# A QKV block on one core: where an image is split, where raw heads lie, and who writes the constants

## The reference, cut to what matters

```python
x = x + _L0_conv_ref(_ln_c(x), w_qkv, w_proj, temperature)
# in it, for each head:
qkv = einsum('oc,bcs->bos', w_qkv, xf)      # q, k, v of 32 channels for each of 8 heads
q, k = _l2norm(q), _l2norm(k)
attn = softmax(einsum('bhsd,bhtd->bhst', q, k) * temperature)
out = einsum('bhst,bhtd->bhsd', attn, v)
```

## Time and profile before

| | |
|---|---|
| median of 3 runs | 2443.84 us |
| the profiled execution: its own time | 2460.1 us |
| its span | 2458.3 us |
| busy share of the span | PE 82%, DVE 84%, ACT 71%, POOL 26% |
| granted TensorE clock, mean over the span | 0.904 of full |
| TensorE's first projection to its last, about | 24 to 134 us |
| first scores of the attention | 167.58 us |

### The profile page before, as it was taken

How to read it: one execution, slowest core, us unless ns; L and a number is a source line. 1 busy time by engine, 2 the same in 40 slices (tenths; PEclk the granted TensorE clock), 3 DMA queues, 4 the chain that set the end, 5 groups by cost and what they waited for, 6 DMA issues and landing times. The chain is left out here.

```text
span 2458.3 us, 84235 instructions
## 1 busy us (share of the span) xinstructions
PE 2004.6 (82%) x28694; PEld 1522.9 (62%) x28695; DVE 2066.0 (84%) x3804; ACT 1751.1 (71%) x2771; POOL 635.1 (26%) x604
## 2 busy tenths in 40 slices
PE   6649999999999999999996307865897209999995
PEld 3327666666666666666665205652586209999995
DVE  5879999999999999999997746768798547888883
ACT  5669999999999999999994524546687426666662
POOL 3431111111111111111110463440164642333331
PEclk9869999999999999999998558995898559999997
DMA  2013232323232323232332233434022452223235
GB/s 82 1 34 91 74 89 73 90 73 90 72 91 72 91 71 91 71 92 71 92 89 73 83 126 116 116 93 146 30 69 76 160 177 46 49 47 49 50 49 152
DMA packets 296697, 203.12 MB, mean 83 GB/s; under 512 B 153587, under 2 KB 277958, under 8 KB 296358
## 3 DMA queue, kind: packets, MB, share of 16 engines
q1 hardware_dynamic: 275840, 163.70, 24.5%
q0 software_dynamic: 19776, 35.73, 5.6%
q10 hardware_dynamic: 998, 2.62, 0.3%
HBM read 64.79 MB, written 112.92 MB: 72 GB/s over the span
## 5 line engine op out<-in xcount | busy, mean ns | idle before, releaser
L595 DVE TENSOR_TENSOR plow<-prob 128x1024 f16<-128x1024 f32 (+1 forms) x1024 | 1128.1, 1173 | 4.7 <-ACT prob L506 4.7
L506 ACT ACTIVATE prob<-scores 128x1024 f32<-128x1024 f32 x1024 | 998.9, 1026 | 91.3 <-PE scores L638 63.6
L658 PEld LDWEIGHTS outp<-vs,prob 128*128 128x128 bf16 x7680 | 516.1, 98 | 277.9 <-issue 215.8
L658 PE MATMUL outp<-vs,prob 128*128 (+1 forms) x7680 | 604.2, 193 | 27.2 <-DVE plow L595 16.5
L638 PE MATMUL scores<-qT,kT 128*128 (+1 forms) x2048 | 611.6, 380 | 7.6 <-DMA kT<-shift_rows 2.7
L660 PE MATMUL outp<-vs,plow 128*128 (+1 forms) x7680 | 601.6, 193 | 0.0
L660 PEld LDWEIGHTS outp<-vs,plow 128*128 128x128 f16 x7680 | 503.3, 97 | 59.8 <-issue 0.6
L448 POOL TENSOR_TENSOR osum<-osb 128x128 f32<-128x128 f32 x64 | 85.8, 1341 | 968.3 <-DVE rec L600 968.3
L1527 POOL DMA_INDIRECT token_sums<-m1eyo,m1edest x71 | 132.4, 1864 | 292.9 <-DMA token_sums<-m1eyo,m1edest 183.6
L1370 PE MATMUL m1eph<-m1exT,m1ew1c 128*128 128x128 f16 x3408 | 204.3, 220 | 1.7 <-issue 1.7
L1370 PEld LDWEIGHTS m1eph<-m1exT,m1ew1c 128*128 128x128 f16 x3408 | 195.4, 99 | 2.4 <-ACT m1exT L1407 1.9
(11 more groups left out here) (398 smaller groups left out, 3375.2 us busy)
## 6 DMA issues: line engine op xcount, KB each, us to landing
sorted_rows<-zero SPq DMA_DIRECT2D x128, 522.0 KB, 5.0
staged<-qk SPq DMA_DIRECT2D x73, 128.0 KB, 2.3
m0exr<-sorted_rows SPq DMA_DIRECT2D x71, 130.5 KB
m1exr<-sorted_rows SPq DMA_DIRECT2D x71, 130.5 KB, 2.5
ls_got<-expert_rows SPq DMA_DIRECT2D x8, 1024.0 KB, 5.7
na_staged<-in_L_ffn_W_dram SPq DMA_DIRECT2D x16, 512.0 KB, 3.7
m1dstg<-in_L_ffn_W_dram SPq DMA_DIRECT2D x16, 512.0 KB
tok<-in_x_dram SPq DMA_DIRECT2D x8, 512.0 KB, 8.2
```

What stands on the lines that cost most here:

```text
L506: act.activation(prob[g % PBUF][:, :], scores[g % 2][:, :], ACT.Exp, scale=1.0 / (QK_SCALE * QK_SCALE)).then_inc(prob_ready, 1)
L595: dve.tensor_tensor(l[:, 0:n], p[:, 0:n], high(p)[:, 0:n], ALU.subtract).then_inc(low_ready, 1)
L658: pe.matmul(to, high(prob[g % PBUF])[:, cols], v, start=(g == 0 and i == 0 and j == 0), stop=False, skip_group_check=True)
```

## The change

1. The two blocks of constants are gone. Their GpSimd work is done at the start of `make_qkv`'s block, together with `zero` and the quarter of `qT`, now filled by one memset of 8192 elements a row. `qT`, `shift_rows` and `zero` are allocated outside the attention. VectorE makes `shift_rows` between the weights' centring and their split, and `tau` is loaded ahead of the image.
2. `raw` and `sq` no longer have memory of their own: they lie in the image's place. So all eight chunks must be split before the first `take`. ScalarE waits for `xl_ready` to reach `NG`.
3. `x_high` and `x_low` have left the loop. `heads_high(g - 1)` stands between tile 1 and tile 2 of group g.
4. The exponential's table is loaded by an instruction at the end of the block and no longer at the start of the attention.
5. In `layer1_start` the seven DMAs go from ScalarE's queue to the front of SyncE's.

```diff
-        raw = [sb(f"raw{u}", [P, GT, QK]) for u in range(2)]
-        sq = [sb(f"sq{u}", [P, GT, QK]) for u in range(2)]
+        image = xc[:, :, :].rearrange("p k s -> p (k s)").rearrange("p (n t c) -> p n t c", n=4, t=GT)
+        raw = [image[:, u] for u in range(2)]
+        sq = [image[:, 2 + u] for u in range(2)]
...
             sp.dma_start(wn[:, :, :], w_dram.rearrange("(m p) c -> p m c", p=P)).then_inc(w_in, 16)
+            sp.dma_start(tau[:, :], temp_dram.rearrange("h a b -> (h a b)").partition_broadcast(P)).then_inc(t_in, 16)
             for g in range(NG):
                 sp.dma_start(xc[:, :, chunk(g)], src[:, :, chunk(g)]).then_inc(x_in[g], 16)
-            sp.dma_start(tau[:, :], temp_dram.rearrange("h a b -> (h a b)").partition_broadcast(P)).then_inc(t_in, 16)
...
-            for g in range(EARLY):
-                x_high(g)
+            x_high(0)
             for n, (k, m0, m1) in enumerate(W_PARTS):
                 act.wait_ge(w_turned, n + 1)
                 act.activation(wh[:, k, m0 * P:m1 * P], pt[n % 2][:, 0:(m1 - m0) * P], ACT.Copy, scale=W_SCALE
                                ).then_inc(w_high, 1)
+                if n % 2:
+                    x_high(n // 2 + 1)
+            for g in range(3, NG):
+                x_high(g)
             act.wait_ge(made, 1)
             root(0)
+            act.wait_ge(xl_ready, NG)
             for g in range(NG):
                 if g >= 2:
                     act.wait_ge(q_low, (g - 1) * GT)
                     act.wait_ge(ss_ready, g - 1)
                 for i in range(GT):
+                    if g and i == GT // 2:
+                        heads_high(g - 1)
                     take(g, i)
                 if g + 1 < NG:
                     root(g + 1)
-                if EARLY <= g + 3 < NG:
-                    x_high(g + 3)
-                if g:
-                    heads_high(g - 1)
                 norms(g)
             heads_high(NG - 1)
+            act.activation(warm[:, :], tau[:, 0:1], ACT.Exp)
...
+            dve.wait_ge(t_in, 16)
+            dve.tensor_scalar(shift[:, :], tau[:, :], -1.0, None, ALU.mult).then_inc(shifted, 1)
...
+                pool.wait_ge(set_up, 10)
+                pool.memset(qT[3 * DH:4 * DH, :], QK_SCALE / DH).then_inc(set_up, 1)
+                pool.wait_ge(set_up, 11)
...
             pool.memset(vs[:, :, :, 2 * DH:VW], 1.0).then_inc(made, 1)
-            for g in range(EARLY):
+            constants()
+            for g in range(NG):
                 x_low(g)
             for g in range(NG):
-                if EARLY <= g + 3 < NG:
-                    x_low(g + 3)
                 heads_low(g)
```

More of the change, by code:

```diff
@@ L61, in clear_semaphores, with make_qkv @@
     nc.all_engine_barrier()
[L64 to L80, removed]
+def make_qkv(nc, x_dram, w_dram, temp_dram, ident32, ident16, consts, xc, wn, tau, qk, vs, qT, shift_rows, zero):
     assert QK_SCALE == W_SCALE
@@ L88, in make_qkv @@
     NV = 4
-    EARLY = 3
+    below, ones, steps, first, tile_no, tok2, base = consts
     ctx = ExitStack()
@@ L120, in make_qkv @@
         made = sem("made")
+        ident_zero = sem("ident_zero")
+        ident_done = sem("ident_done")
+        set_up = sem("set_up")
+        shifted = sem("shifted")
         xh_ready = sem("xh_ready")
@@ L276, in _ @@
                 dve.tensor_scalar(wn[:, m, :], wn[:, m, :], wmean[:, m:m + 1], None, ALU.add).then_inc(w_cent, 1)
+            dve.wait_ge(t_in, 16)
+            dve.tensor_scalar(shift[:, :], tau[:, :], -1.0, None, ALU.mult).then_inc(shifted, 1)
+            dve.wait_ge(shifted, 1)
+            dve.tensor_tensor(shift[:, :], shift[:, :], tau[:, :], ALU.max).then_inc(shifted, 1)
+            dve.wait_ge(shifted, 2)
+            dve.tensor_scalar(shift[:, :], shift[:, :], -1.0, P_SHIFT * LN2, ALU.mult, ALU.add).then_inc(shifted, 1)
+            dve.wait_ge(shifted, 3)
+            dve.tensor_scalar(shift_rows[3 * DH:4 * DH, :, :], shift[3 * DH:4 * DH, :].unsqueeze(2)
+                              .broadcast_to([DH, HEADS, CHUNK]), QK_SCALE, None, ALU.mult).then_inc(shifted, 1)
             for n, (k, m0, m1) in enumerate(W_PARTS):
@@ L310, in _ @@
+            pool.memset(ident32[:, :], 0.0).then_inc(ident_zero, 1)
+            pool.memset(ident16[:, :], 0.0).then_inc(ident_zero, 1)
+            pool.wait_ge(ident_zero, 2)
+            for m in (ident32, ident16):
+                pool.affine_select(out=m[:, :], in_=m[:, :], compare_op=ALU.not_equal, fill=1.0,
+                                   base=0, pattern=[[-1, P]], channel_multiplier=1).then_inc(ident_done, 1)
             pool.memset(vs[:, :, :, 2 * DH:VW], 1.0).then_inc(made, 1)
-            for g in range(EARLY):
+            constants()
@@ L364, in _, with attention @@
                     turn(g + 2)
-def attention(nc, qk, vs, tau, ident16, aout, sorted_rows):
+def attention(nc, qk, vs, ident16, aout, sorted_rows, qT, shift_rows, zero):
     ctx = ExitStack()
@@ L457, in _ @@
             pool.sem_inc(osb_used, 1)
-            pool.wait_ge(shift_set, 1)
-            for n in range(QCONST):
-                c = slice(n * 2 * S // QCONST, (n + 1) * 2 * S // QCONST)
-                pool.memset(qT[3 * DH:4 * DH, c], QK_SCALE / DH).then_inc(q_const, 1)
-            pool.wait_ge(q_const, QCONST)
             pool.memset(vfull[:, :, :, DH:DH + 1], 1.0).then_inc(vfull_set, 1)
@@ L480, in _ @@
         def _(act):
-            act.activation(warm[:, :], tau[:, 0:1], ACT.Exp)
             for j in range(NCH):
@@ L574, in _ @@
                 dve.sem_inc(placed[u], 16)
-            dve.tensor_scalar(shift[:, :], tau[:, :], -1.0, None, ALU.mult).then_inc(shift_ready, 1)
-            dve.wait_ge(shift_ready, 1)
-            dve.tensor_tensor(shift[:, :], shift[:, :], tau[:, :], ALU.max).then_inc(shift_ready, 1)
-            dve.wait_ge(shift_ready, 2)
-            dve.tensor_scalar(shift[:, :], shift[:, :], -1.0, P_SHIFT * LN2, ALU.mult, ALU.add).then_inc(shift_ready, 1)
-            dve.wait_ge(shift_ready, 3)
-            dve.tensor_scalar(shift_rows[3 * DH:4 * DH, :, :], shift[3 * DH:4 * DH, :].unsqueeze(2)
-                              .broadcast_to([DH, HEADS, CHUNK]), QK_SCALE, None, ALU.mult).then_inc(shift_set, 1)
             def take_turned(turn, u):
@@ L2215, in build @@
             wn = flat[:, NT * HEADS * 2 * DH - WN:NT * HEADS * 2 * DH].rearrange("p (m c) -> p m c", c=D)
-            make_qkv(nc, x, w_qkv, temperature, ident32, ident16, image, wn, tau, qk, vs)
-            attention(nc, qk, vs, tau, ident16, image, sorted_rows)
+            make_qkv(nc, x, w_qkv, temperature, ident32, ident16, consts, image, wn, tau, qk, vs, qT, shift_rows, zero)
+            attention(nc, qk, vs, ident16, image, sorted_rows, qT, shift_rows, zero)
         project_attention(nc, x, w_proj, image, ident32, tok, stats)
```

83 lines of the change are left out of this document (34 added, 49 removed).

## The result

The changed kernel took 2436.39 us (median of 18 runs, 2433.09 to 2443.88) against 2442.66 (18 runs, 2436.66 to 2450.08) of the kernel before on the same chip: a ratio of 0.9974, 95% interval 0.9964 to 0.9983. So it is 6 us faster, half of what I called the bound for telling a change, but measured twice. My sum said +1.7 us. The traced execution of the kernel before (2460.1 us) lies above all 18 of its runs here and among those on the other chips (2453.78 to 2472.84), while that of the changed kernel (2435.69) lies among its 18.

The account below looks back on a forecast made before the run. No engine was full in the loop; ScalarE's takes waited for GpSimd and TensorE. QKV block +3.3, attention's start -2.0 and layer 1 +0.4 gave +1.7 us: 2445.5 on the runs' median, range 2433.5 to 2452.5, with scatter 2455.

Parts of the forecast that it names:

- the bound for telling a change: Whole kernel: 0.5% (12.2 us), about what a measurement can tell from no change.
- The start: QKV block up to the first `take`: it comes at 41.0, 15.0 us later than before.
- The first four takes: QKV block, group 0: given 8.10 us, not the 5.9 that group 0 took at full clock.
- A round: QKV loop, norms to norms: 3.45 + 4.12 + 1.33 + 4.19 = 13.1 us; the seventh 11.5.
- The attention's start: Eight turns ahead of the attention: 10.3 us in place of 12.32, without memsets holding VectorE's copies; -2.0 us.
- Layer 1: Layer 1's start: SyncE's rows up to 3.8 us later, weights sooner; bounds 0 and +2, taken as +0.4 us.
- the sum of the QKV block: QKV block: last group's line 266 at 145.25 against 141.92, nothing changed from there to the block's end; +3.3 us.
- both rivals together: No lock at the start and no held units in the loop: 2432.6 us; chance 0.10.
- The rival that the lock does not bite at the start: Start: weights centred before the memset ends, low halves done at 35.1, 5.9 us less: 2439.6; chance 0.20.
- the one on the units: Loop: scalings not held by GpSimd, four take 2.50 us, round 12.1, 7 us less: 2438.5; chance 0.14.
- the rival of still later weights: Start: `tau` delays the image or centring is held six times; up to 4 us more, 2449.5; chance 0.06.
- the clock rival: Loop: TensorE stays at 1.2 GHz after pauses, 17.3 us a round, 2475 us, slower; chance 0.08.

Follow-up runs that it names:

- the run with the memset late: Changed kernel with the long memset of `qT` moved behind the image's last low half; ratio 0.9967 to the kernel before.
- the order alone: Kernel before with only the rounding of the heads moved between the second and third tile of the next group; ratio 0.9952 to the kernel before.

## Why the prediction was wrong

The sum said +1.7; the traces say -4.1 against the mean of the kernel before (3.8 at the first scores, 0.3 in layer 1), the time -6.3. By its own steps:

- **The start.** "+15.0 us" was 13.2. The mechanism is as written: the hold of the means' scaling to the memset's end, the held centring, then GpSimd's pace. Two sizes were off: the memset (8.2 for 6.92) and with it all that follows, and GpSimd's last low half at 39.1 for 41.0.
- **The first four takes.** I gave 8.10 because TensorE had stood idle; they took 6.96 (39.16 to 46.12), 1.1 us less. Two tiles were ready both times; the difference is the clock behind the third. In the earlier trace rows the fourth take came 2.90 us after the third, here 1.95, as in the second trace of the kernel before (56.40 to 58.35), where the clock was 1.00 from 56 us. Windows of the kernel before, then of the changed one (granted clock third from the right):

```profile
56.00:58.00 2.00, 2.00 (x9) 1.04 (x8) 1.03 (x3) 1.36 (x3) 0.00 (x0) 0.58 0.00 0
```

```profile
44.00:46.00 2.00, 2.00 (x16) 1.23 (x14) 0.35 (x1) 1.45 (x3) 0.00 (x0) 1.00 0.00 0
```

- **A round.** 13.1 was 12.85. Each part is where I put it: 3.30 us from norms to line 260 (76.00 to 79.30, forecast 3.45), four scalings in 3.46 held once, 4.1 from the first scaling to the last rounding's end (79.30 to 83.43). Over six rounds the quarter microsecond makes 1.5 us. These three make the 4.6 us by which line 260 came before my 145.25.
- **The reference.** I compared with line 266 at 141.92 in one trace. In the three others it starts at 143.16, 143.26 and 144.37. Another 1.3 us against the mean. My sum took one execution's QKV block for the kernel's, though the three different rounds in it were there to read.
- **The attention's start.** -2.0 was -1.1 to -1.4. The eight turns took 10.61 us, 1.7 less, as forecast but 0.3; the first turn came 3.87 us behind GpSimd's last heads and not 3.33, for which I have no cause (3.4 to 3.6 in the other traces of both kernels). The table load in its new place was over at 146.05, while GpSimd worked on to 147.30, so it cost nothing, as forecast.
- **Layer 1.** +0.4 was -0.3. The rows came 2 us later, the upper bound of my range, but the table load no longer stood behind the weights, and the next group more than made up for it.

The step that failed is thus the sum of the QKV block, "+3.3 us", which measured -2.5 against the mean of four traces (-1.3 against the one): three terms too long by 1.8, 1.1 and 1.5 us, all on one side, beside a reference that was 1.3 short. The first takes came 12.5 us later than the mean of before, and from there to line 260 the changed kernel gained 15: a tenth of either is more than 1 us, against a net of 2.5.

The time alone would have misled: 2436.39 lies nearer to either single rival (2439.6 and 2438.5) than to my 2445.5, and within the recorded range, though the traces rule both rivals out. That it fell within the range is luck. The range's text says that it reaches to both rivals together, but its lower end, 2433.5, lies above their 2432.6.

The rival that the lock does not bite at the start is out (3.89 us where 0.17 would do, and the run with the memset late), and so is the one on the units (3.46). The weights were centred at 15.13 (11.12 + 4.01), sooner than my 16.8, so the rival of still later weights is out too. The clock did fall in the loop at times. Windows of the changed kernel (columns as in the earlier trace rows):

```profile
70.00:72.00 2.00, 0.39 (x3) 0.26 (x4) 0.76 (x3) 2.00 (x5) 2.00 (x2) 1.00 0.00 0
82.00:84.00 2.00, 0.40 (x8) 0.22 (x4) 1.55 (x3) 1.20 (x3) 2.00 (x3) 1.00 0.00 0
84.00:88.00 4.00, 3.54 (x12) 1.68 (x13) 2.35 (x3) 2.29 (x6) 2.00 (x2) 0.60 0.00 0
98.00:102.00 4.00, 4.00 (x17) 1.99 (x15) 3.14 (x5) 1.44 (x6) 0.85 (x1) 0.57 0.00 0
```

A granted clock of 0.60 and 0.57 means that most of these 4 us passed at 1.2 GHz, and the rounds were 12.85 all the same: TensorE has slack in them. So the clock rival's price is out, but my argument against its condition was wrong too: I held that the clock falls only behind a pause of some 5 us, and here it fell right behind 2 us in which TensorE still worked 0.40. Twelve us earlier it had worked 0.39 of 2 and kept the full clock. What decides it, these rows don't show.

In the run with rounds of 11.2 (memset late, rounding behind tile 3) the slack ends: in the one of 12.34 ScalarE waited 1.05 us for TensorE ahead of the third take. The Trainium skill (SBUF — State Buffer, section "Who interferes with whom") says that a VectorE instruction which uses both ports, as `tensor_scalar` can, and a GpSimd one lock each other out for a whole instruction, whichever was first. The traces agree, in both directions: on VectorE 3.89 us for 0.17; on GpSimd, in the run with the memset late, 4.38 us for the first pair of low halves (2.79 in the changed kernel), beside VectorE's 2.29 us for `shift_rows`:

```profile
9.86 2.29 DVE L278 TENSOR_SCALAR shift_rows<-qkv_shift 32x4096 f16<-32x4096 f32 x1
```

```profile
10.43 4.38 POOL L304 TENSOR_TENSOR qkv_xl<-tok,qkv_xh 128x512 f16<-128x512 f32 x2 [6.35 <-ACT qkv_xh L155]
```


What I didn't ask is what the order alone would do. My account of a round had its parts: its 4.19 us from the fourth take to the norms hold ScalarE's wait for the sum of squares, 2.56 us in the trace, long enough for the image's 2.05. The new order and the rest (early split, constants and memset ahead, image's place) came in one change, and I summed them together: -14.9 us for the order and +11 for the rest (153.92 to 165.07). In time the order alone gave 12 us, all of the change 6.

## What to carry to other kernels

Cost each part of a bundled change by itself, with the others undone: here one moved call gave more than all of the gain, and the early split with the long memset lost most of it again. Work that an engine does in the shadow of a wait was nearly free here (0.4 us a round for the image's 2.07); ahead of the loop it was paid in full. Try every place for the last group's rounding in the next group's order: in the kernel before a round was 15.3 to 16.9 us with it behind tile 4, 13.24 behind tile 2 and 11.6 behind tile 3, in the changed kernel 13.69, 12.85 and 11.2. And keep long GpSimd instructions away from the small VectorE steps on which a start hangs. When a forecast is a small difference of two large terms, read the reference from more than one execution.

## What the runs showed of the hardware

GpSimd's addition of two halves in the attention (`osum`) stands beside VectorE's stream of sixteen instructions without a gap. In most iterations it takes 1.36 us; in 21 of 64 of the first trace of the changed kernel, and in none of its second, it took 11.04. Both cost nothing: the iterations stay at 17.6 us. In the four traces of one chip there were 14 to 21 such long ones in 64, in the eight of two others 0 or 1; whether the chip decides it is not tested. In one iteration each of two other runs it took a whole stretch of the stream, as here with the memset late:

```profile
1262.94 15.58 POOL L474 TENSOR_TENSOR osum<-osb 128x128 f32<-128x128 f32 x1 [14.94 <-DVE rec L603]
```

```profile
1262.79 15.41 DVE L598 TENSOR_TENSOR plow<-prob 128x1024 f16<-128x1024 f32 x14
1280.77 0.69 DVE L598 TENSOR_TENSOR plow<-prob 128x512 f16<-128x512 f32 x1 [2.57 <-ACT prob L521]
```

ScalarE could not empty the next outputs until GpSimd was done, VectorE ran dry, TensorE paused, and this iteration and the next took 34.9 us in place of 17.6 + 12.6. So some 4.6 us of a single execution can come from one such wait, in a stage that no edit touched. That GpSimd waited for SBUF, and wasn't slow for another reason, is my reading of its end, just behind the stream's; what decides it I did not test. The Trainium skill (SBUF — State Buffer, section "Who interferes with whom") says that a VectorE instruction with two SBUF inputs contends with a GpSimd one that reads SBUF; that agrees, and the traces add that, by this reading, the wait can outlast fourteen such instructions.
